# Projections in thirds, one third in each slot of an attention kernel; turned tiles in a bank of their own

## The chip, the cores and the metric

One core of one Trainium2 chip. The metric is the device time of one execution in microseconds (us). Engines are named as in the profile: PE (TensorE), DVE (VectorE), ACT (ScalarE), POOL (GpSimd), SP (SyncE, which here only issues transfers).

## What is computed

A gated cross-attention block and a gated feed-forward block behind it, all in float32. Cut to what matters here:

```
q = concat(ctx, layernorm(x)) @ Wq              # B=8, T=256, 1024 -> 512: 32 heads of 16
k = layernorm(x) @ Wk ; ssm_k = ctx @ Wsk       # 8 key heads, each for G=4 query heads
v = layernorm(x) @ Wv ; ssm_v = ctx @ Wsv
s = q @ [ssm_k, k].T / 4 + alibi, masked to the last 64 positions, of both kinds of keys
x = x + tanh(g_xattn) * (softmax(s) @ [ssm_v, v] @ Wo)
x = x + tanh(g_ffn) * ffn(layernorm(x))         # router, top 4 of 128, 8 blocks of gate/up, shared part
```

## The kernel before

Each float32 operand of a product is split into two parts, `hi` and `lo`, and each product is done in three passes (`PASSES`: hi x hi, lo x hi, hi x lo). ACT makes the high half by a copy, DVE or POOL the low half by a subtraction. So a projection tile is 12 or 24 products on PE.

All engines follow one order written out by hand: a loop over slots, `for n in range(SLOTS)`. A batch has 32 slots (`UNITS`), 4 (`NB`) for each of 8 groups of heads. In slot n PE makes the scores of unit n (`scores`, tile `ps_scores`), and 14 slots later (`LAG`) the same scores turned (`scores_turned`, `ps_scoresT`) for the softmax; DVE takes the row maxima (`maxima`, `neg_max`), which PE turns (`turn_max`) in the third slot after a group's last, which ACT copies (`max_out`, `max_rows`) and sends into the last rows of `q_stack` (`stack_max`). ACT takes the exponentials. The products with the values (`times_v`, tile `ps_o`, 32 small ones) come in every fourth slot. DVE turns their result (`o_turn`, `o_blocks`), POOL divides by the sums.

The work for the next batches hangs on constants that name a slot relative to a batch's first: `PREP` turns rows of ctx and of the normalised x on PE (`prep`, 4 tiles a batch; halves by `prep_high` and `prep_low`, the latter DVE's `actT_lo`), `K_PROJ`, `Q_PROJ` (4 tiles of 24 products), `V_PROJ`, `TURN_V`, `TIMES_WO` (2 tiles of 12 products of 512 columns, one batch later), `TURN_X` (the new x, called x1, turned for the feed-forward part). Each of these jobs takes one of the two banks of `ps_proj` in turn (`take_bank`), and waits until the job two before has been read out (semaphore `pj_done`). `scores(n)` waits for the maxima of slot n - 2 (`max_done`).

Keys and queries then go to where the scores read them: `keep_k` and `keep_q` write them to DRAM (`k_kept`, `q_kept`; each is three transfers, one for each pass), and `stack_k`, `stack_q` read them into `k_stack` and `q_stack` in another layout. Only groups 0 and 1 of batch 0 go directly from `qT` to `q_stack` (`stack_q_first`, `DIRECT = 2`). The other rows of the stacks are written once, by ACT (`key_rows_out`, `query_rows_out`), for groups 3 to 7 in slots 0 to 8 (`FILL_ROWS`). The queries of batch 1 are projected in slots 3, 6, 9 and 12.

The first batches' projections stand ahead of the loop; their weights are split in twelve pieces (`halves`) as they arrive, ten low halves on DVE and two on POOL. From slot `END` = 256 on the feed-forward part follows.

## Time and profile before

| | us |
|---|---|
| median of 3 runs | 975.49 (972.8 to 976.08) |
| profiled execution | 969.84 |
| its span, first to last instruction | 968.0 |
| PE busy | 905.6 (94%) |
| DVE / POOL / ACT busy | 568.6 / 486.6 / 408.3 |
| mean granted clock of PE | 0.991 of full speed |

The profile is of one execution, the runs are timed apart. Busy time of PE counts overlapping matmuls as drawn, so a busy PE isn't one at its peak. A line number is that of the instruction, which can stand in a helper: L1574 is every product of `product`, L1653 the scores, L1672 the turned scores, L1685 the products with the values.

### The profile page before, as it was taken

The page shows a single profiled execution, that of the slowest core. Times are in us where ns is not written, and L with a number is a line of the kernel's source. Part 1 is how long each engine was busy: PE and PEld are TensorE (multiplying, and loading weights), DVE is VectorE, ACT ScalarE, POOL GpSimd, SP SyncE. Part 2 cuts the span into 40 slices and gives each one's busy share as a digit, 9 for nine tenths or more (in the row PEclk, how much of TensorE's full clock was granted, in tenths as well). Part 3 has the DMA queues.
Part 4 walks back from the last instruction along what each step waited for, and adds up shares of the span by engine and source line. Part 5 has one row for each costly group of instructions (what it writes and reads, how often), then busy time and mean ns, then how long its engine had stood idle before and what let it go on. Part 6 is the DMA issues. An engine that isn't in the chain of part 4 may idle for free.

```text
span 968.0 us, 17729 instructions
## 1 busy us (share of the span) xinstructions
PE 905.6 (94%) x6744; PEld 773.7 (80%) x6744; DVE 568.6 (59%) x1117; ACT 408.3 (42%) x858; POOL 486.6 (50%) x531
## 2 busy tenths in 40 slices
PE   6869999999998999989998998899999999999998
PEld 6768978888887989867786786678888888888886
DVE  5357575666667575666122673865655556565657
ACT  4655444353544444454401514334443444444431
POOL 1123061513324151316120999965778888887841
PEclk9899999999999999999999999999999999999999
DMA  6695567473847565499010114450111111202036
GB/s 225 172 188 166 124 163 200 130 202 114 203 125 207 115 171 145 138 254 278 2 44 0 44 44 154 140 183 27 66 66 44 66 54 34 87 22 66 23 98 250
DMA packets 80422, 117.01 MB, mean 121 GB/s; under 512 B 6345, under 2 KB 49098, under 8 KB 79306
## 3 DMA queue, kind: packets, MB, share of 16 engines
q1 hardware_dynamic: 78592, 115.11, 41.9%
q8 instruction: 54, 0.88, 0.4%
q10 hardware_dynamic: 1746, 0.77, 0.4%
q14 instruction: 30, 0.25, 0.1%
HBM read 77.13 MB, written 37.81 MB: 119 GB/s over the span
## 4 chain that ended last, share of the span: by engine, by line
PE 79%; DVE 10%; DMA 3%; issue 3%; ACT 2%; POOL 2%; SPq 1%; ACTq 0%; DVEq 0%; POOLq 0%
PE ps_proj L1574 19%; PE ps_scores L1873 18%; PE ps_scoresT L1873 9%; PE ps_scores L1574 6%; PE ps_o L1685 5%; PE ps_proj L1873 4%; PE ps_scores L1653 4%; PE ps_scoresT L1574 4%; PE ps_scoresT L1672 4%; DMA q_stack<-max_rows 2%; DVE actT_lo L1208 2%; DVE neg_max L1243 2%; DVE o_blocks L1261 1%; DMA q_kept<-qT_hi 1%; PE ps_o L1574 1%
## 5 line engine op out<-in xcount | busy, mean ns | idle before, releaser
L1243 DVE TENSOR_REDUCE neg_max<-ps_scores 128x2 f32<-128x384 f32 (+1 forms) x256 | 128.6, 513 | 136.4 <-PE ps_scores L1653 134.6
L925 ACT ACTIVATE probsT<-ps_scoresT 128x512 f32<-128x512 f32 (+1 forms) x256 | 134.8, 542 | 148.1 <-PE ps_scoresT L1672 144.7
L1653 PE MATMUL ps_scores<-k_stack,q_stack 114*128 114x192 f32 (+1 forms) x512 | 104.8, 289 | 11.5 <-DVE neg_max L1243 7.9
L1134 ACT ACTIVATE part_sums<-ps_scores 128x512 f32<-128x512 f32 x96 | 57.5, 599 | 130.8 <-PE ps_scores L1873 130.8
L1672 PE MATMUL ps_scoresT<-q_stack,k_stack 116*128 116x256 f32 x448 | 103.9, 303 | 9.0 <-DMA q_stack<-max_rows 6.7
L1653 PEld LDWEIGHTS ps_scores<-k_stack,q_stack 114*128 114x128 f32 x512 | 80.4, 193 | 24.9 <-DVE neg_max L1243 15.7
L674 POOL TENSOR_TENSOR o_normal<-o_blocks,inv_sums 128x128 f32<-128x128 f32 x64 | 25.8, 404 | 147.7 <-DVE inv_sums L1263 147.7
L809 POOL TENSOR_TENSOR w_expert_lo<-w_sums,w_expert_hi 128x256 fp32r<-128x256 f32 x64 | 63.8, 1009 | 45.5 <-ACT w_expert_hi L1054 45.5
L821 POOL TENSOR_TENSOR big<-big,basis 128x512 f32<-128x512 f32 x56 | 77.5, 1402 | 14.9 <-DVE basis L1524 14.9
L1672 PEld LDWEIGHTS ps_scoresT<-q_stack,k_stack 116*128 116x128 f32 x448 | 71.5, 194 | 12.3 <-DMA q_stack<-max_rows 7.6
L680 POOL TENSOR_TENSOR oT_lo<-oT_raw,oT_hi 128x256 fp32r<-128x256 f32 x32 | 23.6, 736 | 110.5 <-ACT oT_hi L934 110.5
L1685 PE MATMUL ps_o<-probsT,v_ones 128*32 128x128 f32 (+1 forms) x2048 | 64.2, 267 | 0.5 <-issue 0.5
L1574 PE MATMUL ps_proj<-actT_hi,wq_hi 128*128 128x256 f32 x224 | 64.7, 289 | 0.0
L1574 PE MATMUL ps_proj<-actT_lo,wq_hi 128*128 128x256 f32 x224 | 64.0, 286 | 0.0
L1574 PE MATMUL ps_proj<-actT_hi,wq_lo 128*128 128x256 f32 x224 | 63.9, 285 | 0.0
L1515 DVE TENSOR_TENSOR basis<-part_sums,silu_gate 128x512 f32<-128x512 f32 x32 | 24.2, 756 | 67.2 <-ACT silu_gate L1142 67.2
L1685 PEld LDWEIGHTS ps_o<-probsT,v_ones 128*32 128x32 f32 x2048 | 53.5, 112 | 9.5 <-issue 1.0
L1524 DVE TENSOR_TENSOR basis<-basis,big 128x512 f32<-128x512 f32 x56 | 57.2, 1021 | 1.0
L1494 DVE TENSOR_TENSOR part_sums<-part_sums,ps_scoresT 128x512 f32<-128x512 f32 x32 | 22.0, 688 | 53.6 <-ACT part_sums L1134 53.6
L809 POOL TENSOR_TENSOR w_expert_lo<-w_raw,w_expert_hi 128x256 fp32r<-128x256 f32 x48 | 46.3, 978 | 7.1 <-ACT w_expert_hi L1054 7.1
L1873 PE MATMUL ps_scores<-xnT_hi,w_expert_hi 128*128 128x512 f32 x128 | 49.8, 389 | 0.0
L1873 PE MATMUL ps_scores<-xnT_hi,w_expert_lo 128*128 128x512 f32 x128 | 49.8, 389 | 0.0
(265 smaller groups left out, 2549.7 us busy)
## 6 DMA issues: line engine op xcount, KB each, us to landing
k_stack<-k_kept SPq DMA_DIRECT2D x64, 192.0 KB, 5.2
q_stack<-q_kept SPq DMA_DIRECT2D x31, 384.0 KB, 5.4
q_kept<-qT_hi SPq DMA_DIRECT2D x16, 512.0 KB
big<-coeff_rows SPq DMA_DIRECT2D x8, 1024.0 KB, 4.7
xn_rows<-in_x SPq DMA_DIRECT2D x8, 512.0 KB, 4.2
k_kept<-kT_hi SPq DMA_DIRECT2D x16, 256.0 KB
q_kept<-qT_lo SPq DMA_DIRECT2D x8, 512.0 KB
x_rows<-in_x SPq DMA_DIRECT2D x8, 512.0 KB, 5.3
```

The lines of the kernel that those rows point to most:

```text
L674: pool.tensor_tensor(ON[:, p % 2, :, odd * D:(odd + 1) * D], OB[:, n % 2, :, 0:D], RI[:, n % 2].unsqueeze(2).broadcast_to([P, T // 32, D]) ...
L809: pool.tensor_tensor(WS[n % 2]["lo"][:, w, :], w_source(n, w), WS[n % 2]["hi"][:, w, :].bitcast(F32), ALU.subtract).then_inc(e_lo, 1)
L821: pool.tensor_tensor(dst, dst, BS[:, j, :], ALU.add).then_inc(acc_done, 1)
L925: act.activation(PT[:, g % 2, 2 * j:2 * j + blocks].rearrange("p h f r w -> p (h f r w)"), ST[:, n % 2, 0:blocks].rearrange("p h n -> p (h ...
L1134: act.activation(TP[:, u % 2, j, :], src[:, u % 2, :], ACT.Copy).then_inc(taken, 1)
L1243: dve.tensor_reduce(NM[:, g % 2, 2 * i:2 * i + 2], SA[:, n % 2, :, 0:keys], AX.X, ALU.max, negate=True).then_inc(max_done, 1)
L1524: dve.tensor_tensor(dst, BS[:, j, :], cB[:, k % 2, group_columns(t)], ALU.mult).then_inc(basis_done, 1)
L1574: ins = pe.matmul(out, stat(s, c), mov(m, c), start=c == cs[0] and j == 0, stop=c == cs[-1] and j == PARTS - 1)
L1653: ins = pe.matmul(SA[:, n % 2, f, 0:2 * (near.stop - near.start)], QS[0:TOP, g, i, f].rearrange("p r w -> p (r w)"), keys[:, near, :].rear ...
L1672: ins = pe.matmul(ST[:, n % 2, v, :], KS[0:ROWS, g, j + v, 1 - v].rearrange("p w s -> p (w s)"), QS[0:ROWS, g, j + v].rearrange("p f r w - ...
L1685: ins = pe.matmul(PO[32 * r:32 * r + 2 * D, j * W:j * W + cols_j], VA[:, j, g, :], PT[:, n % 2, 2 * j:2 * j + cols_j // W, :, r, :].rearra ...
L1873: ins = pe.matmul(bank[:, u % 2, :], WS[n % 2][s][:, w, c * P:(c + 1) * P], operand(MEETS[w], m, c, g), start=first and c == 0 and j == 0, ...
```

## The change

K, V, each query tile and each Wo tile are cut into three parts (`third`, `keys_values_third`), and the tables give each part a slot of its own, so that in full batches each of the 24 slots without products with the values has one part. The context is handed over turned (a transposition of the input array on the host), so that ctx needs no `prep`; its halves are made by ACT (`ctx_high`) and POOL (`ctx_low`; DVE for batches 0 and 1). Everything that PE turns (`prep`, `turn_v`, `turn_x`) now uses one bank `PT_`, the former bank of the turned maxima, with a semaphore `turn_done` (batches 0 and 1 use a bank of `ps_proj` beside it); the turned maxima `PM` go into the second half of the bank of `ps_o`, with two new waits. All groups of batch 0 are stacked directly. The rows of the stacks are written by ACT and POOL ahead of the loop. DVE's statistics of x1 come one slot after the residual. The last batch keeps its Wo tiles whole. PE begins with seven products on a tile of ones (`warm`).

```diff
-LOAD_ROWS, STATS = -59, (-46, -45)
-PREP, K_PROJ, Q_PROJ, V_PROJ = (-32, -31, -30, -29), (-27, -26), (-24, -22, -19, -16), (-7, -5)
+LOAD_ROWS, STATS = -64, (-51, -50)
+CTX_HIGH, CTX_LOW = (-44, -43), (-43, -42)
+PREP, K_PROJ, V_PROJ = (-42, -38), (-35, -34, -32), (-15, -14, -12)
+Q_PROJ = ((-31, -30, -28), (-27, -26, -24), (-23, -22, -20), (-19, -18, -16))
+LEAD = (PV - NM_TURN) // NB + 1
-TURN_V, TIMES_WO, TURN_X = 15, (52, 55), (62, 63)
+TURN_V, TIMES_WO, LAST_WO = 16, ((53, 54, 56), (57, 58, 60)), ((52,), (55,))
+def x_turn_slot(b, t):
+    return (69, 72)[t] if b < B - 1 else (62, 64)[t]
...
-    PO, PM = POB[:, 0, :], PNM[0:4 * NB, 1, 0:P]
+    PO, PM = POB[:, 0, :], POB[0:4 * NB, 1, 0:P]
+    PT_ = PNM[:, :, :].rearrange("p h n -> p (h n)")
...
+        def third(out, stat, mov, count, part):
+            steps = [(c, s, m) for c in range(count) for s, m in PASSES]
+            size = len(steps) // 3
+            for i in range(part * size, (part + 1) * size) if part is not None else range(len(steps)):
+                c, s, m = steps[i]
+                ins = pe.matmul(out, stat(s, c), mov(m, c), start=i == 0, stop=i == len(steps) - 1, skip_group_check=True)
+            return ins
...
+        def warm():
+            ones = VA[:, 0].rearrange("p g e -> p (g e)")
+            pe.wait_ge(ones_set, 1)
+            for _ in range(WARM):
+                pe.matmul(PJ[:, 1, 0:T], ones[:, 0:P], ones[:, 0:T], start=True, stop=True)
+
+        def take_turn(*job):
+            kind, b, t = job
+            if kind == "prep" and b < 2 and t == 1:
+                if b == 1:
+                    pe.wait_ge(pj_done, passed("v", 0, 0))
+            elif TURNS[job] >= 1:
+                pe.wait_ge(turn_done, TURNS[job])
+            return turn_place(*job)
...
         def turn_max(n):
             pe.wait_ge(nm_lo, n + 1)
             if n >= 1:
                 pe.wait_ge(nm_out, n)
+            if n > LEAD - 1:
+                pe.wait_ge(o_turned, n - LEAD + 1)
...
         def times_v(n):
-            pe.wait_ge(pj_done, passed("turn_v", b, 0))
+            pe.wait_ge(turn_done, passed("turn_v", b, 0))
             pe.wait_ge(exp_done, NB * (n + 1))
             if n >= 1:
                 pe.wait_ge(o_turned, n)
+            pe.wait_ge(nm_out, min(n + LEAD, GROUPS))
...
+        warm()
         keys_values("k", 0, 0)
-        first_queries(range(HC))
-        prep(0, 2)
-        prep(0, 3)
-        keys_values("k", 0, 1).then_inc(k_mm, 1)
+        first_queries(range(HC - 1))
+        for t in range(TB):
+            prep(0, t)
+        first_queries(range(HC - 1, HC))
+        keys_values("k", 0, 1)
+        for i in range(2):
+            keys_values("v", 0, i)
         first_queries(range(HC, 2 * HC))
...
-        for g in range(DIRECT):
+        for g in range(HK):
             stack_k(0, g)
             stack_q_first(g)
-        keep_q(0)
+            if g == 3:
+                for n in range(FIRST_O, len(halves)):
+                    weight(n)
                 keep_k(1)
...
+    ctx = np.asarray(inputs["ctx_2048"]).transpose(0, 2, 1).reshape(B, HC, P, T)
+    inputs["ctx_2048"] = ctx.transpose(0, 2, 1, 3)
```

How the order moves at three places. First PE, where a batch begins in the slot loop, before: three slots of the four with a `prep` each (`ctx_rows` and `xn_rows` turned into `ps_proj`), no products of a projection between.

```order
L1597 MATMUL ps_proj<-ident,ctx_rows 128x128 [waits ctx_in,pj_done]
L1597 MATMUL ps_proj<-ident,ctx_rows 128x128 x3
L1653 MATMUL ps_scores<-k_stack,q_stack 128x192 [waits max_done]
L1653 MATMUL ps_scores<-k_stack,q_stack 128x192
L1672 MATMUL ps_scoresT<-q_stack,k_stack 128x256 [waits exp_done]
L1597 MATMUL ps_proj<-ident,ctx_rows 128x128 [waits ctx_in,pj_done]
L1597 MATMUL ps_proj<-ident,ctx_rows 128x128 x3
L1653 MATMUL ps_scores<-k_stack,q_stack 128x192 [waits max_done]
L1653 MATMUL ps_scores<-k_stack,q_stack 128x192
L1672 MATMUL ps_scoresT<-q_stack,k_stack 128x256 [waits exp_done,max_in5]
L1672 MATMUL ps_scoresT<-q_stack,k_stack 128x256
L1662 MATMUL ps_o_max<-ident,max_halves 16x128 [waits nm_out,nm_lo]
```

After, one whole slot, 26 of a batch ahead, and the first rows of the next (`wo_hi`, `wo_lo` by `oT_hi`, `oT_lo` are products with Wo, four to a third; `ps_o_max` is now the turned tiles' bank, and the turned maxima go to `ps_o`).

```order
L1781 MATMUL ps_scores<-k_stack,q_stack 128x192 [waits max_done]
L1781 MATMUL ps_scores<-k_stack,q_stack 128x192
L1802 MATMUL ps_scoresT<-q_stack,k_stack 128x256 [waits exp_done,max_in3]
L1802 MATMUL ps_scoresT<-q_stack,k_stack 128x256
L1792 MATMUL ps_o<-ident,max_halves 16x128 [waits o_turned,nm_out,nm_lo]
L1712 MATMUL ps_o_max<-ident,xn_rows 128x128 [waits xn_done,turn_done]
L1712 MATMUL ps_o_max<-ident,xn_rows 128x128 x3
L1676 MATMUL ps_proj<-wo_hi,oT_lo 128x512
L1676 MATMUL ps_proj<-wo_lo,oT_hi 128x512
L1676 MATMUL ps_proj<-wo_hi,oT_hi 128x512
L1676 MATMUL ps_proj<-wo_hi,oT_lo 128x512
L1781 MATMUL ps_scores<-k_stack,q_stack 128x192 [waits max_done]
```

The four turned tiles became two, which stand four slots apart, and a third of a projection now stands behind one of them in the same slot.

Second DVE, at the same place before: its queue has a low half `actT_lo` between the maxima of each of four slots.

```order
L1208 TENSOR_TENSOR actT_lo<-ps_proj,actT_hi 128x4x128 [waits prep_hi]
L1243 TENSOR_REDUCE neg_max<-ps_scores 128x2 [waits s_mm]
L1269 STREAM_TRANSPOSE oT_raw_73<-o_normal 128x256 [waits oT_lo,o_done]
L1208 TENSOR_TENSOR actT_lo<-ps_proj,actT_hi 128x4x128 [waits prep_hi]
L1243 TENSOR_REDUCE neg_max<-ps_scores 128x2 [waits s_mm]
L1208 TENSOR_TENSOR actT_lo<-ps_proj,actT_hi 128x4x128 [waits prep_hi]
L1250 CAST max_halves<-neg_max 128x8 [waits nm_t,max_done]
L1252 TENSOR_TENSOR max_halves<-neg_max,max_halves 128x8 [waits nm_hi]
L1243 TENSOR_REDUCE neg_max<-ps_scores 128x2 [waits nm_lo,s_mm]
L1261 STREAM_TRANSPOSE o_blocks<-ps_o 128x256 [waits o_done,pv_mm]
L1263 RECIPROCAL inv_sums<-o_blocks 128x8 [waits o_turned]
L1208 TENSOR_TENSOR actT_lo<-ps_proj,actT_hi 128x4x128 [waits prep_hi]
```

After, from the slot of the first Wo residual on (`x_rows` is the residual, `x_stats` its statistics).

```order
L1324 TENSOR_REDUCE neg_max<-ps_scores 128x2 [waits s_mm]
L1358 SCALAR_TENSOR_TENSOR x_rows<-ps_proj,tanh_gates,x_rows 128x512 [waits wo_mm,x1_in]
L1324 TENSOR_REDUCE neg_max<-ps_scores 128x2 [waits s_mm]
L1350 STREAM_TRANSPOSE oT_raw_74<-o_normal 128x256 [waits oT_lo,o_done]
L1364 BN_STATS x_stats<-x_rows 128x6 [waits pj_done]
L1366 BN_AGGR x_mean_var<-x_stats 128x2 [waits x1_st]
L1324 TENSOR_REDUCE neg_max<-ps_scores 128x2 [waits s_mm]
L1289 TENSOR_TENSOR actT_lo<-ps_o_max,actT_hi 128x4x128 [waits prep_hi]
L1331 CAST max_halves<-neg_max 128x8 [waits nm_t,max_done]
L1333 TENSOR_TENSOR max_halves<-neg_max,max_halves 128x8 [waits nm_hi]
```

The low halves `actT_lo` moved four slots apart, and the residual's statistics moved behind the maxima of the next slot.

Third SP's queue of transfers ahead of the loop, before: groups 0 and 1 go directly, then all queries are spilled and the others read back.

```order
L476 DMA k_stack<-k_kept 48x4x256 [waits k_rows_set,pad_kept,k_kept]
L483 DMA q_stack<-qT_hi 16x1024 [waits q_rows_set,pj_done]
L483 DMA q_stack<-qT_lo 16x1024
L483 DMA q_stack<-qT_hi 16x1024
L466 DMA q_kept<-qT_hi 8x16x1024 [waits pj_done]
L466 DMA q_kept<-qT_lo 8x16x1024
L466 DMA q_kept<-qT_hi 8x16x1024
L494 DMA q_stack<-q_kept 48x2x1024 [waits q_rows_set,q_kept]
L476 DMA k_stack<-k_kept 48x4x256 [waits k_rows_set,pad_kept,k_kept] x2
L460 DMA k_kept<-kT_hi 8x16x512 [waits pj_done]
L460 DMA k_kept<-kT_hi 8x16x512
```

After, the same place, from group 1 on.

```order
L527 DMA k_stack<-k_kept 48x4x256 [waits rows_pool,pad_kept,k_kept]
L534 DMA q_stack<-qT_hi 16x1024 [waits rows_pool,pj_done]
L534 DMA q_stack<-qT_lo 16x1024
L534 DMA q_stack<-qT_hi 16x1024
L527 DMA k_stack<-k_kept 48x4x256 [waits rows_act,pad_kept,k_kept]
L534 DMA q_stack<-qT_hi 16x1024 [waits rows_act,pj_done]
L534 DMA q_stack<-qT_lo 16x1024
L534 DMA q_stack<-qT_hi 16x1024
```

The spill and the loads back of batch 0 are gone; each group now has one load of keys and three of queries.

## Rows read from the trace of the kernel before

**Rows 1.** The page, part 1: busy time by engine, share of the span, instructions.
```profile
PE 905.6 (94%) x6744; PEld 773.7 (80%) x6744; DVE 568.6 (59%) x1117; ACT 408.3 (42%) x858; POOL 486.6 (50%) x531
```

**Rows 2.** Windows cut at each 32nd slot: stretch, length, busy by engine, clock, DMA.
```profile
core 0: us, PE busy (x) PEld busy (x) DVE busy (x) ACT busy (x) POOL busy (x), PEclk, DMA share, GB/s
0.00:40.70 40.70, 29.86 (x200) 28.12 (x201) 19.41 (x36) 22.40 (x41) 7.88 (x20) 0.96 0.68 203
...
40.70:87.60 46.90, 36.77 (x357) 33.46 (x355) 26.38 (x66) 27.31 (x60) 12.78 (x16) 0.93 0.74 184
...
195.60:249.90 54.30, 51.23 (x583) 46.49 (x582) 35.19 (x91) 24.29 (x55) 17.83 (x28) 1.00 0.61 162
...
412.70:455.90 43.20, 37.03 (x423) 31.15 (x422) 27.17 (x74) 22.18 (x52) 15.55 (x24) 0.92 1.04 271
...
455.90:968.00 512.10, 494.65 (x2292) 402.02 (x2290) 286.88 (x400) 191.08 (x377) 349.31 (x312) 1.00 0.22 73
```

**Rows 3.** Timeline of PE, the scores that open five slots: start us, us, instruction.
```profile
208.47 0.44 PE L1653 MATMUL ps_scores<-k_stack,q_stack 114*128 114x128 f32 x2
...
211.89 0.37 PE L1653 MATMUL ps_scores<-k_stack,q_stack 114*128 114x192 f32 x2
...
212.24 0.36 PE L1653 MATMUL ps_scores<-k_stack,q_stack 114*128 114x192 f32 x2
...
215.68 0.37 PE L1653 MATMUL ps_scores<-k_stack,q_stack 114*128 114x192 f32 x2
...
217.14 0.44 PE L1653 MATMUL ps_scores<-k_stack,q_stack 114*128 114x128 f32 x2
```

**Rows 4.** Chain of waits, three runs of PE in that batch: start us, us, what.
```profile
209.19 2.86 PE ps_proj L1574 x24
...
236.08 2.99 PE ps_proj L1574 x12
...
247.45 0.44 PE ps_proj L1699 x4
```

**Rows 5.** The same chain, the first of four DVE passes on turned tiles.
```profile
252.41 0.52 DVE actT_lo L1208
```

**Rows 6.** DVE by line, 195.6 to 249.9 us: xcount, busy us, mean ns, idle before.
```profile
L1243 DVE TENSOR_REDUCE neg_max<-ps_scores 128x2 f32<-128x384 f32 (+1 forms) x32 | 16.2, 514 | 18.2 <-PE ps_scores L1653 18.1
...
L1208 DVE TENSOR_TENSOR actT_lo<-ps_proj,actT_hi 128x512 fp32r<-128x512 f32 x4 | 2.7, 664 | 0.0
```

**Rows 7.** Timeline of PE: two early products, then the first scores.
```profile
10.32 0.41 PE L1574 MATMUL ps_o<-actT_hi,wkv_lo 128*128 128x256 f32 x1
...
10.53 0.41 PE L1574 MATMUL ps_o<-actT_lo,wkv_hi 128*128 128x256 f32 x1
...
40.74 0.59 PE L1653 MATMUL ps_scores<-k_stack,q_stack 114*128 114x128 f32 x4
```

**Rows 8.** Timeline of SP's queue: direct load; last spill of queries, first load back, twice.
```profile
34.08 0.58 SPq L483 DMA_DIRECT2D q_stack<-qT_hi  x1
...
38.68 2.66 SPq L466 DMA_DIRECT2D q_kept<-qT_hi  x1
...
49.54 0.34 SPq L494 DMA_DIRECT2D q_stack<-q_kept  x1
...
228.11 0.61 SPq L466 DMA_DIRECT2D q_kept<-qT_hi  x1
...
241.12 0.33 SPq L494 DMA_DIRECT2D q_stack<-q_kept  x1
```

**Rows 9.** Chain of waits in batch 0, on the turned maxima's transfer.
```profile
60.51 10.16 DMA q_stack<-max_rows
```

**Rows 10.** The page, part 6: transfers, xcount, KB each, us to landing.
```profile
q_stack<-q_kept SPq DMA_DIRECT2D x31, 384.0 KB, 5.4
...
q_stack<-qT_hi SPq DMA_DIRECT2D x4, 64.0 KB, 3.3
```

**Rows 11.** Timeline of ACT, the copy of the turned maxima in the slot from 212.24.
```profile
213.40 0.25 ACT L910 ACTIVATE max_rows<-ps_o_max 16x128 fp32r<-16x128 f32 x1
```

More of the change, by code:

```diff
@@ L567, in _ @@
             if s == 1:
[L568 removed]
+                sp.wait_ge(q_kept, 16 * PARTS * (B - 1))
                 router = cols(a["L0_ffn_w_router"], 0)
@@ new lines, in keys_values_third, with queries @@
+        def keys_values_third(job, b, part):
+            size = 2 * HC * PARTS // 3
+            for src in range(2):
+                steps = range(max(part * size - src * HC * PARTS, 0), min((part + 1) * size - src * HC * PARTS, HC * PARTS))
+                if len(steps):
+                    keys_values(job, b, src, steps)
+        def queries(b, r, part):
+            dst = take_bank("q", b, r) if part == 0 else place("q", b, r)
+            ins = third(dst[:, 0:T], lambda h, c: WQ[h][:, c, r * P:(r + 1) * P], lambda h, c: AT[h][:, c, :], 2 * HC, part)
+            if part == 2:
+                ins.then_inc(q_mm, 1)
@@ L1688, in times_v, with times_wo @@
             ins.then_inc(pv_mm, 1)
-        def times_wo(b, t):
-            dst = take_bank("wo", b, t)
-            pe.wait_ge(oT_lo, HC * (b + 1))
-            product(dst, lambda h, c: OT[h][:, t, c, :], lambda h, c: WO[h][:, c, :], range(HC)).then_inc(wo_mm, 1)
+        def times_wo(b, t, part):
+            first = part in (0, None)
+            dst = take_bank("wo", b, t) if first else place("wo", b, t)
+            if first:
+                pe.wait_ge(oT_lo, HC * (b + 1))
+            ins = third(dst, lambda h, c: OT[h][:, t, c, :], lambda h, c: WO[h][:, c, :], HC, part)
+            if part in (2, None):
+                ins.then_inc(wo_mm, 1)
         def turn_x(b, t):
-            dst = take_bank("x", b, t)
+            dst = take_turn("x", b, t)
             pe.wait_ge(x1_n, TB * b + t + 1)
```

465 lines of the change are left out of this document (252 added, 213 removed).

## Prediction

> **What bounds the kernel now.** I read the page's busy times first. PE is busy for 94% of the span, every other engine for 59% or less [rows 1], so time can only come from PE: from work taken off it, from its gaps, or from its slow clock. The windows then say where the gaps are [rows 2]. I cut them at every 32nd slot, since a batch has 32 slots. From 455.9 us on (512.1 us, PE 97% busy) the diff moves almost nothing, and no gain is to be had. The head, 0 to 40.7 us, has PE busy for 29.86. Batch 0's slots, 40.7 to 87.6, have 36.77 of 46.90. From 87.6 to 412.7 the batches are alike: 54.3 us, PE 51.23 (one stands in the rows, six there are, 325.1 us together). Batch 7's slots take 43.2 with 37.03 busy, at a clock of 0.92.
>
> A busy PE in such a row isn't PE at its peak, because a matmul that waits in the pipe is drawn longer. So I price a slot from the starts of its first scores [rows 3]. Where products stand between (208.47 to 211.89) the slot takes 3.42 us, of which the 24 products are 2.86 [rows 4]: 0.56 is left. The next slot has no product, 0.35. The next, with 24 products and the turned maxima, is 3.44, so 0.58 without them. The fourth, with the products with the values (PV below), is 1.46. That is 2.95 for a group of four slots, 23.6 for a batch. Here PE was never held up. A batch has 24 products for the keys, 24 for the values, 96 for the queries: 144 at 2.86/24 = 0.119 us are 17.2. The 24 with Wo, twice 2.99 in the chain [rows 4], are 6.0. Turned tiles cost 0.44 each [rows 4]; there are seven (four `prep`, the values, two of x1), 3.1. Sum 49.9. Against 54.3, 4.4 us of each batch is waiting. The chain shows for what: four low halves `actT_lo` in a row on DVE [rows 5], each 664 ns beside 514 ns for a slot's `neg_max` [rows 6]. Slots without products are too short for DVE, which then stands idle for 18.2 us of the batch in the long ones [rows 6]. Work is badly spread, it isn't too much.
>
> **The change part by part.**
> *Thirds.* A group has three slots without PV, a batch 24; and K, V, four queries and two Wo tiles in thirds are 24 pieces, one for each. A third of 8 products is 0.95 us, one of Wo's about 1.0. So slots become 1.3 to 1.55 us, and PV's stays at 1.46. DVE has 35.2 us in a batch [rows 2], 1.10 a slot. Its worst new slot (13: maxima, a query's low half, one tile's row statistics) I put at 1.8, the 0.51 and two passes like the 0.66 [rows 6], the next at 1.4; PE asks for the maxima of two slots back, so 0.3 over is hidden. If that cover were gone, each such slot would cost its 0.3, some 1 us a batch.
> *Context turned ahead.* Two `prep` a batch go, 2 x 0.44 = 0.9 us of PE, with ACT's and DVE's two passes from PSUM. In their place ACT reads SBUF, and POOL makes the low half (it has 17.8 of 54.3 us busy; hidden).
> So a batch needs 49.9 - 0.9 = 49.0. I take 49.5 for slots that still meet a wait now and then: 4.8 us off each of five batches, 4.2 off batch 1 (53.7 now, no x1 to turn): **28**. Bounds: 49.0 for all (31), or half of the waits kept, 51.5 (17).
> *Turned tiles in a bank of their own.* Spaced by three slots or more (5, 8, 16, 22, 26), each is emptied by DVE in 0.66 us [rows 6] and by ACT in about as much, long before the next, 4 us later; nothing.
> *Maxima turned into the bank of PV.* `turn_max` now waits for the DVE transpose two slots earlier, and PV for ACT's copy of the maxima turned in the slot before. That copy ended at 213.65 [rows 11], 1.41 us after its slot began at 212.24. In the new order PV stands at 1.53 + 0.46 = 1.99. So 0.6 is left: nothing. If ACT came late, all of PE's queue would stand behind PV, in each of 64 groups.
> Here a rule speaks against the change. The Trainium skill, "PSUM — Partial Sum Buffer", section "PSUM bank collisions raise a hardware error", says that two engines must never be in one bank and quadrant at once and that the hardware doesn't make them take turns, so whoever shares a bank between two uses has to pay in waits on semaphores. The trace of before has each use in its own bank and can't show that price; by the rows it is 0 and the sum stays, by the rule it can be anything that ACT's lateness makes it, which is rival 5.
> *Spill.* From the first spill of the queries to the first load back 13.0 us pass in a batch (228.11 to 241.12), with SP standing in between [rows 8]; the load lands 5.4 later [rows 10]. The spill starts in slot 18 as before. 13.0 + 5.4 = 18.4 us, and slot 32, which needs the load, comes 14 x 1.5 = 21 us after slot 18. It fits by 2 to 3 us, and SP's other work is queued behind.
>
> *Head.* Two of the first products start 0.21 us apart [rows 7], against 0.119 later: the slow level, 1.2 GHz, after PE's waiting. Seven products on ones run before, while nothing else could. 23 products at 0.094 less are 2.2 us. Until the first scores PE now has 168 products, 20.0, and four turned tiles, 1.8, from about 7.2 us: 29.0 if nothing held it. The splits of twelve weight pieces on ACT and then DVE, and x's statistics and normalisation through POOL, do hold it; I add 4.5, between nothing and the 9 that now lie in 0 to 40.7 (PE idle for 10.8 of it [rows 2]), so 33.5 against 40.74 [rows 7]: **7**. Bounds 30 and 38.
> *Batch 0.* The queries no longer go by DRAM: before, 10.9 us lie between last spill and load [rows 8]; a direct load lands in 3.3 [rows 10]. But there are 24 of them and 8 of the keys, at 0.58 us of SP each [rows 8]: 2.4 a group of four slots, faster than the slots need. The four Wo loads and the spill of batch 1's keys come after group 3, some 5 us, and group 4 just makes its slot. ACT's five sets of rows leave these slots. The transfer of the maxima that took 10.16 [rows 9] no longer competes with a spill. PE's own work: slots 0 to 13, ten thirds 9.5 and scores 3.9; slots 14 to 31, 4.5 groups 13.2, seven thirds 6.7, three turned tiles 1.3, and 0.9 for eight slots without a piece, where DVE sets the pace (27.17/32 = 0.85 a slot [rows 2]). 35.5, and 2.5 for transfers: 38 against 46.9: **9**. Bounds 36 and 44.
> *Batch 7.* Wo of batch 6 was 6.0 in two blocks; in slots with DVE as pace its six pieces hide 1.7 behind it. The x1 tiles of batch 6 move behind slot 256, 0.9 here and there: **2**. With DMA at 1.04 of its engines' time [rows 2] another stall may take it.
>
> Sum 28 + 7 + 9 + 2 = **46 us**. The profiled execution is 968.0 + 1.84 = 969.84, the median of the runs 975.49; its lowest is 972.8. I expect 924 for a profile and 975.5 - 46 = 929.5 for the median.
>
> **The rivals.**
> 1. *Forecast*: PE becomes the pace of each slot, 929.5, with 919 to 942 as its range. Chance 0.70.
> 2. *The slots stay paced by hand-offs*: equal slots leave each engine the right mean, but scores wait for maxima in most groups. For: DVE and PE hand over twice a slot. Against: 1.10 of 1.5 us. They give back a third of what is there, 52.5 us a batch: 10 instead of 28 off, 947.5. Chance 0.14.
> 3. *The spilled queries come late*: DMA's share was 0.61 and must rise to 0.67. If spill and load stretch by a third (6 us) against 2 spare, that is 4 a batch for six batches, 24 of the 46 lost: 953.5. Against: the lag grows only if DMA is near its limit, and 0.67 isn't. Chance 0.06.
> 4. *The head is bound by transfers*, weights and stacks, and gives nothing: 16 less, 945. For: share 0.68 and 0.74. Against: 10.9 us of spill go. Chance 0.06.
> 5. *Slower*: PV waits for the copy of the maxima in each of 64 groups. ACT has one queue with exponentials and high halves ahead. It decides from 46/64 = 0.7 us a group, so the copy must come 1.3 us later than 1.41; at 1 us it is 994. Against: ACT is busy 24.3 of 54.3. Chance 0.04.
>
> **How the numbers follow.** This kernel's measurement tells about 0.3%, 3 us, from no change. All but rival 5 are faster beyond it: 0.95; within it 0.02, for a mixture near its threshold; slower 0.03. The likeliest gives 929.5. Its own range is 919 (31 + 11 + 11 + 3 = 56 off) to 942 (22 + 4 + 6 + 1 = 33 off: all four terms near their low bounds). To hold 8 in 10 I go from 918 up to 949, into rivals 2 and 4; above stay rivals 3 and 5, and half of 2.
>
> **What would show it.** Right: windows of 32 slots at 49 to 50 us; four neighbouring slots between 1.3 and 1.6; first scores near 33.5; slot 32 near 71; `actT_lo` no longer in the chain between slots; early products 0.119 apart. Wrong: `max_rows` or `o_blocks` as what PE waits for before PV or turned maxima; `q_stack<-q_kept` before scores; a clock below 1.00 in the batches; 455.9 to the end longer than 513.

## The result and the profile after

| | before | changed |
|---|---|---|
| median of the runs | 974.14 us (972.66 to 976.08) | 937.94 us (937.33 to 941.46) |
| profiled execution, its span | 969.84, 968.0 | 937.33, 935.5 |
| mean granted clock in it | 0.991 | 0.984 |

The ratio of the medians is 0.9635, with a 95% interval from 0.9603 to 0.9667. That is 36.2 us faster. The forecast was 46 us less, 929.5 us; 937.94 lies in the range given, 8.4 us above the forecast.

Of the changed kernel, first the page's busy times, which answer to [rows 1], then the windows that answer to [rows 2]. They are cut at the first scores, at slot 32, at slot 16 of one of the like batches and the same place of the next, at slot 224, and at the first router product (456.23 us before, 417.88 now).

```profile
PE 888.0 (95%) x6694; PEld 767.0 (82%) x6694; DVE 571.5 (61%) x1107; ACT 401.2 (43%) x838; POOL 519.2 (55%) x562
```

```profile
core 0: us, PE busy (x) PEld busy (x) DVE busy (x) ACT busy (x) POOL busy (x), PEclk, DMA share, GB/s
0.00:36.08 36.08, 29.39 (x199) 27.29 (x200) 22.93 (x38) 22.28 (x41) 22.29 (x35) 0.95 0.64 193
36.08:88.37 52.29, 36.65 (x381) 34.66 (x380) 27.04 (x68) 20.32 (x45) 19.13 (x23) 0.87 0.62 155
184.30:232.71 48.41, 48.41 (x578) 45.43 (x573) 35.03 (x89) 24.58 (x55) 20.35 (x30) 1.00 0.69 182
376.44:417.88 41.44, 36.10 (x429) 30.93 (x423) 29.89 (x79) 22.55 (x52) 16.13 (x25) 0.92 1.04 281
417.88:935.50 517.62, 498.78 (x2297) 405.02 (x2295) 285.66 (x398) 191.28 (x377) 353.20 (x318) 0.99 0.22 74
```

Put beside [rows 2] and the first scores of [rows 7], the 32.5 us that the span lost fall out like this:

| stretch | before | changed | gain | forecast |
|---|---|---|---|---|
| head, to the first scores | 40.74 | 36.08 | 4.7 | 7 |
| slots 0 to 31 | 46.9 | 52.3 | -5.4 | 9 |
| slots 32 to 223 | 325.1 | 288.1 | 37.0 | 28 |
| slot 224 to the first router product | 43.5 | 41.4 | 2.1 | 2 (with its 0.9 behind slot 256) |
| from there to the end | 511.8 | 517.6 | -5.8 | 0 |

A like batch now takes 48.41 us and PE is busy for all of it, where [rows 2] has 51.23 of 54.30. The timeline of PE shows the scores that open the slots of one such group, to be read as [rows 3] was (start us, us, instruction):

```profile
184.30 0.44 PE L1781 MATMUL ps_scores<-k_stack,q_stack 114*128 114x128 f32 x2
185.81 0.36 PE L1781 MATMUL ps_scores<-k_stack,q_stack 114*128 114x192 f32 x2
187.11 0.37 PE L1781 MATMUL ps_scores<-k_stack,q_stack 114*128 114x192 f32 x2
188.63 0.37 PE L1781 MATMUL ps_scores<-k_stack,q_stack 114*128 114x192 f32 x2
190.09 0.44 PE L1781 MATMUL ps_scores<-k_stack,q_stack 114*128 114x128 f32 x2
```

The slots are 1.51, 1.30, 1.52 and 1.46 us long, where one was 3.4 and its neighbour 0.35. In the whole chain of waits from 184 to 233 us PE is the only engine.

What PE waited for in the changed kernel, over the whole span, longest sums first (engine, tile, line, releaser: us in total, times, longest):

```profile
PE ps_scores L1781 <- DVE neg_max L1324: 16.7, 5, 13.2
PE ps_proj L1665 <- DVE down_lo L1515: 6.4, 4, 3.3
PE ps_scoresT L1802 <- ACT probsT L999: 3.1, 6, 1.0
PE ps_scores L1757 <- DVE wq_lo L1279: 2.3, 1, 2.3
PE ps_o L1816 <- ACT max_rows L984: 2.1, 6, 0.7
```

One wait of 13.2 us stands out, in batch 0. Three timelines, PE, DVE and SP's queue, show it from its end to its cause (in brackets the idle time before, and its releaser):

```profile
51.59 0.37 PE L1781 MATMUL ps_scores<-k_stack,q_stack 114*128 114x192 f32 x2
65.39 0.66 PE L1781 MATMUL ps_scores<-k_stack,q_stack 114*128 114x128 f32 x2 [13.18 <-DVE neg_max L1324]
```

```profile
50.29 0.41 DVE L1301 TENSOR_TENSOR second_qT_lo<-ps_proj,second_qT_hi 128x256 fp32r<-128x256 f32 x1
63.89 0.69 DVE L1267 BATCH_NORM_STATS2 stats<-xn_rows 128x6 f32<-128x512 f32 x1 [13.19 <-DMA xn_rows<-in_x]
```

```profile
40.56 3.00 SPq L500 DMA_DIRECT2D w_stage<-in_L_xattn_Wo  x4
43.61 1.32 SPq L511 DMA_DIRECT2D k_kept<-kT_hi  x2
...
59.09 0.59 SPq L534 DMA_DIRECT2D q_stack<-qT_hi  x1
59.72 0.58 SPq L504 DMA_DIRECT2D xn_rows<-in_x  x1
```

PE stands ahead of slot 16 (the scores with 128 columns open a group) for DVE's maxima. DVE stands ahead of its statistics of batch 2, which the change moved from slot 18 to slot 13 of this batch. And the rows that they read are asked for only at 59.72, because the load stands last in SP's queue, behind all 32 stack transfers, the four of Wo and the three that keep the keys of batch 1. SP itself is never idle for long here: it needs 0.62 us from one stack transfer to the next where nothing holds it. The sixteen issues from 45.7 us on took 0.87 us each on average, the longest 2.27.

### The profile page after: what moved, and what is told of

The parts are those of the page before. It is cut to its first block, busy times and chain, and to the rows that moved or that the text cites. A ratio compares the mean times of both kernels' runs of the same rounds, so it can differ in the third digit from the quotient of the medians.

```text
span 935.5 us, 17701 instructions
## 1 busy us (share of the span) xinstructions
PE 888.0 (95%) x6694; PEld 767.0 (82%) x6694; DVE 571.5 (61%) x1107; ACT 401.2 (43%) x838; POOL 519.2 (55%) x562
## 4 chain that ended last, share of the span: by engine, by line
PE 84%; DMA 4%; DVE 3%; POOL 3%; SPq 2%; issue 2%; ACT 1%; POOLq 0%; DVEq 0%; ACTq 0%
PE ps_scores L2004 19%; PE ps_proj L1676 12%; PE ps_scoresT L2004 9%; PE ps_scores L1781 6%; PE ps_scoresT L1802 6%; PE ps_scores L1665 5%; PE ps_o L1816 5%; PE ps_proj L2004 5%; PE ps_proj L1665 5%; PE ps_scoresT L1665 4%; PE ps_proj L1730 4%; SPq L534 1%; DMA q_kept<-second_qT_hi 1%; DMA xn_rows<-in_x 1%; POOL x_normal L757 1%
## 5 line engine op out<-in xcount | busy, mean ns | idle before, releaser
L999 ACT ACTIVATE probsT<-ps_scoresT 128x512 f32<-128x512 f32 (+1 forms) x256 | 137.2, 542 | 149.8 <-PE ps_scoresT L1802 149.4
L1324 DVE TENSOR_REDUCE neg_max<-ps_scores 128x2 f32<-128x384 f32 (+1 forms) x256 | 131.5, 516 | 75.5 <-PE ps_scores L1781 71.2
L1781 PE MATMUL ps_scores<-k_stack,q_stack 114*128 114x192 f32 (+1 forms) x512 | 100.5, 280 | 17.5 <-DVE neg_max L1324 16.7
L1781 PEld LDWEIGHTS ps_scores<-k_stack,q_stack 114*128 114x128 f32 x512 | 82.3, 192 | 28.5 <-issue 14.5
L875 POOL TENSOR_TENSOR w_expert_lo<-w_sums,w_expert_hi 128x256 fp32r<-128x256 f32 x64 | 64.3, 1014 | 45.6 <-ACT w_expert_hi L1130 45.6
L1585 DVE TENSOR_TENSOR part_sums<-part_sums,ps_scoresT 128x512 f32<-128x512 f32 x32 | 22.0, 688 | 52.4 <-ACT part_sums L1210 52.4
```

The lines of the kernel that those rows point to most:

```text
L875: pool.tensor_tensor(WS[n % 2]["lo"][:, w, :], w_source(n, w), WS[n % 2]["hi"][:, w, :].bitcast(F32), ALU.subtract).then_inc(e_lo, 1)
L999: act.activation(PT[:, g % 2, 2 * j:2 * j + blocks].rearrange("p h f r w -> p (h f r w)"), ST[:, n % 2, 0:blocks].rearrange("p h n -> p (h ...
L1324: dve.tensor_reduce(NM[:, g % 2, 2 * i:2 * i + 2], SA[:, n % 2, :, 0:keys], AX.X, ALU.max, negate=True).then_inc(max_done, 1)
L1781: ins = pe.matmul(SA[:, n % 2, f, 0:2 * (near.stop - near.start)], QS[0:TOP, g, i, f].rearrange("p r w -> p (r w)"), keys[:, near, :].rear ...
```

## The experiments

Each is the changed kernel with an edit, timed beside the kernel before. "Slot 16 of a batch" is read from PE's turn of the values, which stands there; in the changed kernel that is at 66.4 us for batch 0 and 112.1 for batch 1.

**e1, the rows of batch 2 asked for earlier.**

```diff
             if g == 3:
+                load_rows(2)
                 for n in range(FIRST_O, len(halves)):
...
-            b = due(n, LOAD_ROWS, 2)
+            b = due(n, LOAD_ROWS, 3)
```

> The changed kernel with one edit: the load of the rows and of ctx of batch 2 is issued on SP behind the fourth group's stack transfers, ahead of the four loads of Wo, and no longer behind all 32 stack transfers. Theory A (batch 0 lost its gain to one stall: DVE stands 13.2 us in the statistics of batch 2, in slot 13, for rows whose load SP's queue issues only at 59.7 us): the load is issued near 41 and has landed by 46, before DVE comes to it at 50.7; the 13.8 us row at slot 12/13 goes, slot 32 starts near 75 in place of 88.4, and the time is 925 us (923 to 928). Theory B (what is behind the stall is late anyway: the last stack transfers, now 1.2 us later, and the spilled queries of batch 1, which stand in the chain at 71.7): part of the wait comes back before slot 32, slot 32 starts at 80 or later, and the time is 930 to 936. Theory C (the place of the load makes nothing, DVE is held by something else): 938.

Measured: 932.53 us (928.24 to 934.24), ratio 0.9578 (0.9546 to 0.9611). The profiled execution was its fastest, with a span of 926.4. The 13.2 us wait is gone, and slot 16 of batch 0 comes at 57.3 in place of 66.4, 9.0 earlier. Theory A has the cause, but not the whole price: another wait came up behind it, as B said. The timeline of PE at the same place:

```profile
51.59 0.42 PE L1803 MATMUL ps_scoresT<-q_stack,k_stack 116*128 116x256 f32 x2
56.32 0.69 PE L1782 MATMUL ps_scores<-k_stack,q_stack 114*128 114x128 f32 x2 [4.31 <-DMA q_stack<-qT_hi]
```

Now group 4's queries themselves are late. The windows of this kernel show the 16 DMA engines with little or nothing free meanwhile:

```profile
40.00:46.00 6.00, 6.00 (x54) 6.00 (x53) 3.99 (x10) 0.77 (x3) 0.00 (x0) 1.00 0.85 257
46.00:52.00 6.00, 4.65 (x39) 4.28 (x37) 2.46 (x7) 3.66 (x8) 4.66 (x4) 1.00 0.95 269
52.00:58.00 6.00, 1.69 (x9) 1.68 (x9) 2.97 (x9) 1.02 (x2) 3.89 (x8) 0.69 0.98 161
```

**e2, the statistics back where they were.** The edit is `STATS = (-46, -45)` in place of `(-51, -50)`.

> The changed kernel with the statistics of batches 2 to 7 five slots later on DVE, where the kernel before has them (offsets -46 and -45), and the load left where it is in SP's queue. Theory A (DVE is only too early for the load): slot 18 comes at 36.1 + 18 x 1.46 = 62.4 us, the rows land at 63.9, so 1.5 us of the 13.2 is left; 926.5 us (925 to 930). Theory B (what is behind the rows, the normalisation and the turned tile in slot 22, is then late instead): the stall moves to PE's wait for xn_rows or for turned tiles in slots 22 to 30 and the time is 931 to 937. If the steady batches need the earlier statistics as well, slots 32 to 223 cost more than 288 us.

Measured: 950.15 us (945.52 to 951.8), ratio 0.9758 (0.9722 to 0.9794): 12 us slower than the changed kernel. In batch 0 it did what A said: DVE waits 2.4 us for the rows in place of 13.2, and slot 16 comes at 55.1. But the like batches take 50.80 us each, two of them 52.4, and over the whole span PE waits six times for the normalised rows, 14.0 us together. The timeline of PE shows the place, the turned tile of slot 22:

```profile
117.11 1.09 PE L1712 MATMUL ps_o_max<-ident,xn_rows 128*128 128x128 f32 x4 [2.19 <-POOL xn_rows L746]
117.85 0.78 PE L1676 MATMUL ps_proj<-wo_hi,oT_lo 128*128 128x512 f32 x1
118.42 0.63 PE L1676 MATMUL ps_proj<-wo_lo,oT_hi 128*128 128x512 f32 x1
```

Since the change turns the tile in slot 22, the statistics must stand as early as they do, or GpSimd's normalisation is late. After the 2.19 us of waiting here PE also runs at its slow level: from 117.1 to 120.6 the granted clock is 0.52. So the early statistics are not a slip: only their load was forgotten.

**e3, the thirds undone.** All three thirds in the slot that holds the last, so K at -32, the queries at -28, -24, -20, -16, V at -12, Wo at 56 and 60.

> The changed kernel with each projection whole again: all three thirds in the slot that now holds the last of them (K at -32, the queries at -28, -24, -20, -16, V at -12, Wo at 56 and 60); DVE's placing, the bank for turned tiles and the loads stay. Theory A (the thirds are what makes the steady batches fast: a whole projection costs PE 2.5 us in one slot while DVE's 1.3 us of maxima a slot can't be caught up in the slots without): six batches take near 325 us as before in place of 288, time 965 to 980. Theory B (the dealing of DVE's work and the bank of its own give it, the thirds little): below 945. Between (each gives a part): 945 to 965; the sum of slots 32 to 223 tells the share.

Measured: 966.57 us (965.78 to 966.66), ratio 0.9933 (0.991 to 0.9956). A like batch takes 52.07 us, of which PE is busy for 50.05. Theory A holds by the time, though slots 32 to 223 take 313 us and not near 325. Without the thirds 3.66 of the 5.86 us that the change takes off each batch (54.27 to 48.41) are gone. The other 2.2 stay, and come from what e3 leaves in: the context that needs no turning, DVE's placing, the bank for turned tiles. No run takes these apart. PE also waits for ACT's copy of the maxima ahead of the products with the values 35 times in e3, 7.8 us together, where the changed kernel has 2.1, so it is beside the thirds that this shared bank is cheap.

**e4, no warm-up.** `WARM = 0` in place of 7.

> The changed kernel with no warm-up products. My prediction's term was 2.2 us saved by them. Theory A (they save nearly that): 940 us, first scores at 38.3. Theory B (PE waits 2.3 us for wq_lo behind the keys' products, the granted clock falls again there and 16 products at 0.21 us follow in either case, so they only save the half speed of the first 12 products, 12 x 0.09 = 1.1 us, which the wait for wq_lo then swallows): 938 us within 0.5, first scores at 36.1 to 36.6.

Measured: 939.69 us (937.62 to 940.1), ratio 0.9652 (0.9623 to 0.9681), not to be told from the changed kernel. The time alone is nearer to A's, but the first scores start at 35.9 us in place of 36.1, so theory B holds for the head, and slot 16 of batch 7 still starts 0.35 us earlier than in the changed kernel. The two profiled executions are 2.5 us apart; all of it comes later, 1.5 between slot 16 of batch 7 and the first router product (21.2 us, 19.7 in the changed kernel) and 1.3 from the shared down projection on, which the edit doesn't touch. In the changed kernel the first twelve products come 0.12 us apart, then PE waits 2.32 us for `wq_lo`, and the products behind it are 0.21 apart again until 14.4:

```profile
7.03 0.36 PE L1730 MATMUL ps_o<-actT_hi,wkv_hi 128*128 128x256 f32 x1 [1.12 <-DVE actT_lo L1284]
11.02 0.58 PE L1757 MATMUL ps_scores<-actT_hi,wq_hi 128*128 128x256 f32 x1 [2.32 <-DVE wq_lo L1279]
```

Without the warm-up the twelve stand 0.21 apart, from 7.14 to 9.62, and the queries' products follow at 9.84 without that wait. Neither order brings the first scores forward.

**e5, the turned tiles close together.** Offsets -39, -38 in place of -42, -38, and 71, 72 in place of 69, 72; the statistics of x1 in the slot of the residual.

> The changed kernel with its thirds, but DVE's work no longer spread: the two turned tiles of a batch stand in neighbouring slots again (offsets -39, -38 and 71, 72 in place of -42, -38 and 69, 72), and the statistics of x1 stand in the slot of the residual. Whole projections gave 52.07 us per batch (before 54.27, changed 48.41), so 2.2 us of the 5.9 gained per batch is not the thirds'. Theory A (it is the spreading of DVE's work): two or three slots of each batch become 0.6 to 1.5 us longer, steady batches at 49.5 to 51, time 946 to 955. Theory B (it is the bank of its own for what is turned and the earlier statistics, and DVE has room in every slot beside thirds): 48.4 to 48.7 per batch, time 937 to 940. Two turned tiles in neighbouring slots share the one bank, so the second one can also wait for DVE's low part of the first: up to 1.4 us a pair, as the pair behind slot 256 shows.

Measured: 959.37 us (958.57 to 960.56), ratio 0.9852 (0.9832 to 0.9873). 51.76 us a batch, 3.35 more and over what A allowed. The waits of PE from 115 to 330 us, some four batches, are these two, and nothing else:

```profile
PE ps_o_max L1708 <- DVE actT_lo L1289: 6.2, 4, 1.5
PE ps_o_max L1830 <- DVE xs_lo L1370: 5.6, 4, 1.4
```

11.8 us in four batches are 2.95 each, nearly the whole loss. The second of two tiles stands behind the first because both use the one bank, and it stands until ACT and then DVE have emptied it. How long that is depends on what DVE has ahead. Here the first tile was turned at 176.89 and ACT had its half at 178.13, but DVE made the low half only behind the residual, its statistics, maxima and a transposition:

```profile
177.42 0.74 DVE L1358 SCALAR_TENSOR_TENSOR x_rows<-ps_proj,tanh_gates,x_rows 128x512 f32<-128x512 f32 x1
179.82 0.65 DVE L1289 TENSOR_TENSOR actT_lo<-ps_o_max,actT_hi 128x512 fp32r<-128x512 f32 x1
```

PE came to the second tile near 179.0 and waited 1.54 us. Had DVE begun at 178.13, the bank would have been free near 178.8, by my estimate, before PE came. In the other pair (the tiles of x1, at 149.0) DVE began 0.5 us behind ACT, and 0.9 of its 1.4 us would be left. So the edit shows the one bank and DVE's lumps together. What either costs alone it doesn't tell.

**e6, the last tile in another bank.**

```diff
+        if job == ("x", B - 1, 1):
+            return PJ[:, JOBS["wo", B - 1, 0] % 2, :]
```

> The changed kernel, with the very last turned tile (x1 of batch 7, second tile) in a free projection bank and not in the one bank for turned tiles. Theory A (of the 6.4 us that the part behind slot 256 costs more than before, 1.4 is PE's wait for the low part of the first tile, because both use one bank): that wait goes, the last router products start 1.4 us earlier, 936.5 us, a difference near what can be measured; the trace shows it as 42.9 to 43.2 us from the first shared product to the last router product in place of 44.5. Theory B (the tiles come no earlier, PE waits for the normalised rows then): 44.5 stays.

Measured: 935.50 us (932.54 to 938.51), ratio 0.9606 (0.9577 to 0.9636). From the first shared product to the last router product 43.4 us pass; the same reading of the changed kernel is 44.9 (that of the expectation ends one product group earlier). By the trace theory A holds; by the times alone this kernel can't be told from the changed one. In the changed kernel each of two steps has its wait, first for the bank, then for the tile:

```profile
475.80 0.60 PE L1834 MATMUL ps_o_max<-ident,x_normal 128*128 128x128 f32 x4
477.81 0.66 PE L1834 MATMUL ps_o_max<-ident,x_normal 128*128 128x128 f32 x4 [1.41 <-DVE xnT_lo L1370]
479.88 0.50 PE L1665 MATMUL ps_scores<-xnT_hi,w_router_hi 128*128 128x512 f32 x1 [1.41 <-DVE xnT_lo L1370]
```

DVE and ACT had nothing else to do here, so 2.0 us from tile to tile, 1.4 of them waiting, is what the one bank costs by itself. In e6 the second tile follows at once:

```profile
475.21 0.60 PE L1838 MATMUL ps_o_max<-ident,x_normal 128*128 128x128 f32 x4
475.65 0.60 PE L1838 MATMUL ps_proj<-ident,x_normal 128*128 128x128 f32 x4
```

**e7, the head reordered.** The load of batch 0's rows behind the first two halves of Wq, and DVE's `weights_low(1)` and `(2)` ahead of its first statistics.

> The changed kernel with the head reordered: the load of batch 0's rows stands behind the first two halves of Wq on SP, and DVE makes the low parts of these two before the statistics of the rows. In the changed kernel PE waits 2.32 us at 8.7 for wq_lo, and its clock falls. Theory A (this wait and the fallen clock are the 2.6 us by which the first scores at 36.1 miss my 33.5): query products start near 9 at 0.12 us apart, first scores at 33.8 to 34.8, time 936. Theory B (the rows, their normalisation and the turned tiles set the head, as the 1.93 us wait for xn_rows at 29.9 and the wait behind the first three query chunks say): the gain is waited away before the turned tile of batch 0 near 17, first scores at 36 or later, time 938 to 939.

Measured: 938.50 us (936.05 to 940.72), ratio 0.963 (0.9599 to 0.9662): no difference. The wait for `wq_lo` is gone and the 36 early query products end at 13.0, but then PE waits for the rows:

```profile
15.28 0.63 PE L1715 MATMUL ps_o_max<-ident,xn_rows 128*128 128x128 f32 x4 [1.95 <-DVE xn_rows L1275]
```

The first scores come at 36.55. Theory B holds: the head goes by the rows' way through statistics, roots, normalisation and splits.

**e8, the queries of batch 0 through DRAM as before** (groups 2 to 7).

> The changed kernel with the queries of batch 0 for groups 2 to 7 taken through DRAM, as the kernel before does, and not straight from SBUF: 18 transfers of 64 KB go, 3 of 512 KB to DRAM and 6 of 128 KB back come. Theory A (what the load of batch 2's rows waits for in SP's queue is the number of issues at about 0.62 us): 18 less, 9 more, so the load is issued 5.6 us earlier and the stall of DVE is 7.5 us in place of 13.2, provided the queries are back in time; slot 16 of batch 0 near 61, time 932 to 934. Theory B (the way through DRAM costs what the kernel before showed, some 10 us until the first queries are back, and SP stands in that wait with everything behind it): PE stands before slot 8 for a query stack, and the stall of DVE is as long as before, time 938 to 944.

Measured: 946.57 us (944.57 to 950.92), ratio 0.9735 (0.9702 to 0.9767), 8.6 us slower than the changed kernel. Theory B has the place, PE's stand for a query stack, but DVE's stall is 9.8 us, between the 7.5 of A and the 13.2 of B, and the time lies 2.6 us above B's range. PE's waits from 36 to 110 us:

```profile
PE ps_scores L1790 <- DVE neg_max L1333: 10.5, 3, 9.8
PE ps_scores L1790 <- DMA q_stack<-q_kept: 6.3, 1, 6.3
```

So the direct transfers are a gain in spite of the stall behind them.

**e9, SP's order by need.** Stacks 0 to 3, Wo, the rows of batch 2, stacks 4 and 5, its context, stacks 6 and 7, and `keep_k(1)` last.

> The first experiment took the stall of DVE away (13.8 us) and brought 9.0 us by slot 16: a 4.3 us wait for the query stack of group 4 came up behind it, with the 16 DMA engines busy 85 to 98 per cent from 40 to 58 us. Here the order on SP is: stacks of groups 0 to 3, Wo, rows of batch 2, stacks of groups 4 and 5, ctx of batch 2, stacks of groups 6 and 7, and only then the keys of batch 1 to DRAM. So 1.25 MB (ctx and the kept keys) no longer stand ahead of group 4. Theory A (what counts is only the bytes and issues ahead of each group's stack): 1.25 MB at the 250 GB/s of that stretch is 5 us, group 4 lands before its slot, slot 16 of batch 0 starts 12 to 13 us earlier than in the changed kernel (53.5 to 54.5), time 924 to 928. Theory B (the DMA engines are full either way, the wait moves to group 5 or 6 or to the kept keys and queries of batch 1): slot 16 of batch 1 stays near 103.5 as in the first experiment, time 930 to 933.

Measured: 934.12 us (933.2 to 934.66), ratio 0.9591 (0.9572 to 0.9611). Slot 16 of batch 0 comes at 54.6, 11.8 us earlier and next to what A expected. But slot 16 of batch 1 comes at 104.2, where e1 had 103.5: B holds, with a time 1.1 us above its range. PE stands 4.0 us shortly ahead of slot 32 for ACT's `probsT`, because ACT stands 5.3 us ahead of the first rounded half of oT, for the second queries to be in DRAM (they lie where oT is written). The chain of waits (start us, us, what):

```profile
63.47 11.63 DMA q_kept<-second_qT_hi
...
75.18 0.10 ACT oT_hi L1015
...
75.50 0.59 ACT probsT L1004
...
76.23 0.77 PE ps_scoresT L1807 x2
```

**e10, that first half six slots later.** `o_high(0)` and `o_low(0)` in slot 33, with e9's order.

> The order on SP of the last experiment (e9), and the first step of batch 0's turned outputs (the rounded half of oT, ACT and GpSimd) six slots later, in slot 33. In e9 ACT stood 5.3 us there, until 75.1, for the second queries to be in DRAM, because they lie where oT is written, and PE stood 4.0 us for probsT behind it. Theory A (that wait is what gave back the gain): no wait for probsT, 46.1 us or less from slot 16 to slot 48 in place of 49.6, time 928 to 931, near 928.5. Theory B (the transfers of this stretch are late altogether, the keys of batch 1 too): another wait in its place, 49 us stay, time 933 to 935.

Measured: 932.85 us (931.06 to 935.97), ratio 0.9594 (0.9571 to 0.9617). Theory B, by the trace: the wait for `probsT` is gone and another is in its place, ahead of slot 32, the first of batch 1, and from slot 16 to slot 48 it takes 51.5 us, more than the 49.6 of e9. SP's queue and PE's timeline:

```profile
60.09 0.61 SPq L519 DMA_DIRECT2D q_kept<-second_qT_hi  x1
...
73.28 0.34 SPq L544 DMA_DIRECT2D q_stack<-q_kept  x1
```

```profile
71.97 0.37 PE L1790 MATMUL ps_scores<-k_stack,q_stack 114*128 114x192 f32 x2
78.16 0.66 PE L1790 MATMUL ps_scores<-k_stack,q_stack 114*128 114x128 f32 x2 [4.67 <-issue]
```

**e11, e10 and e6 together.**

> e10 with the last turned tile in a free projection bank, which took 1.5 us of PE's waits by itself. Expected is e10 less 1.5 us: 926 to 929.5. Rival: the terms don't add, within 0.5 us of e10.

Measured: 930.28 us (926.75 to 932.07), ratio 0.956 (0.9538 to 0.9583). By the medians it is the fastest version, 7.7 us under the changed kernel, and 2.6 under e10, 0.8 above the range expected; e1 (0.9546 to 0.9611) can't be told from it.

**e12, the four small loads behind the queries of batch 1.** `TANH - 20` in place of `TANH - 24`, with e11.

> e11 with the four small loads (gates, amplitudes, scale) issued on SP behind the queries of batch 1 and no longer ahead of them; they take SP's queue 3.9 us, from 57.2 to 61.1. In the four kernels without the first stall (e1, e9, e10, e11) slot 48 starts at 103.5 to 104.7, whatever stands ahead; in e10 and e11 PE stands 4.7 and 6.2 us ahead of slot 32, whose queries went to DRAM at 60 to 65 us, were there at 73.5, and came back near 78. Theory A (the way of the queries of batch 1 through DRAM sets slot 32): they are issued 3.5 us earlier, slot 32 starts 2.5 to 3.5 us earlier (75 to 76 in place of 78.5), slot 48 at 101 to 102, time 927 to 928. Theory B (the stacked keys of batch 1, issued at 65.1 and landed near 74.8, and the full DMA engines set it too): less than 1 us is gained, 929.5 to 930.5.

Measured: 930.43 us (929.05 to 935.56), ratio 0.9571 (0.9544 to 0.9597). The queries are issued 3.9 us earlier, at 57.2, but are back for loading only at 72.4 in place of 73.8; slot 32 starts at 77.3 in place of 78.5. Nearer to B: the way through DRAM has only stretched. It isn't full transfer engines that stretch it: from 58 to 76 us their busy share is 0.61 here, 0.55 in e11 and 0.63 in e10. What holds it is open.

The start of slot 32 of all five without the first stall, from PE's timeline: e1 79.8, e9 80.5, e10 78.2, e11 78.5, e12 77.3, against 88.4 in the changed kernel. Between 8 and 11 us came out of the 13.2, and the medians show only 3.8 to 5.4 of it (e1, e9, e10). In some traces part of the rest is lost in the stretch from slot 16 of batch 6 to the first router product, which all these kernels have alike and where the transfer engines are busy for 0.85 to 0.88. It takes 63.7 us in the changed kernel's trace, 62.6 in e1's, 65.8 in e9's, 64.3 in e10's, and 67.9 in e11's and e12's. The windows of e1 and e12, and PE's longest wait in e12's:

```profile
345.70:408.30 62.60, 56.17 (x672) 48.99 (x671) 46.22 (x121) 32.70 (x75) 19.67 (x32) 0.97 0.88 236
```

```profile
PE ps_scoresT L1815 <- DMA q_stack<-max_rows: 3.2, 1, 3.2
```

```profile
345.10:413.00 67.90, 58.91 (x673) 51.33 (x672) 46.25 (x121) 32.73 (x75) 19.74 (x32) 0.92 0.85 219
```

PE waits up to 3.2 us for the 8 KB of turned maxima in e12's trace and 0.4 in e1's, and the granted clock is 0.92 against 0.97. Executions of one kernel differ by 1.5 us (e9) to 6.5 us (e12), and the differences between the medians of e1, e9, e10 and e12 stay inside that. That this late transfer is what makes them differ is not shown, since each kernel has one trace.

## Why the prediction was right, and where it was not

The main mechanism, thirds that make PE the pace of each slot, is right. That the total lies in the range is in part luck: 9 us too little for the thirds stand against 14.4 too much for batch 0, 2.3 for the head and 5.7 for batch 7 and what follows.

**Thirds, 28: right, and too small; 37.0 measured.** That PE is now the pace is shown by PE busy for 48.41 of 48.41 us, and that the thirds bring most of it by e3 (3.66 of 5.86 us a batch; the rest is not taken apart). The sum of 49.0 was 0.6 too high: a third of Wo took 0.92 to 0.94 and not 1.0, which is 0.4 of it. The 0.5 that I added for slots that still meet a wait wasn't needed. That is 1.1 us in each of the batches from 64 on. Slots 32 to 63 gained 6.2 (53.7 to 47.5) where I took 4.2, and slots 192 to 223 take only 46.90: the tiles and the first two thirds of the keys, which the change moves ahead into the batch before, have no next batch there, 1.5 more. 5.4 + 2.0 + 1.5 is nearly the 9 that the term was short. Rival 2, pace by hand-offs, is out by the same rows. So is rival 3: in the like batches PE waits for no spilled query, with the transfer engines busy for 0.69.

**"Turned tiles in a bank of their own ... nothing": right, on the condition that was named.** Spaced by three slots or more the bank is free in time; in neighbouring slots, with DVE's work in lumps as well, it costs 3.35 us a batch (e5). At the end of the last batch, where I didn't look, nothing spaces them: that is the 1.5 us of e6.

**Rival 5, PV behind the copy of the maxima: 2.1 us.** It is in the list of waits, six times, 0.7 at most, where 0.7 in each of 64 groups would have been needed to lose. The Trainium skill, "PSUM — Partial Sum Buffer", section "PSUM bank collisions raise a hardware error", leaves the keeping apart to the program, so each shared bank is paid for in semaphore waits; the trace agrees, with 2.1 us for PV's bank, and 2.95 us a batch in e5 for the one of the turned tiles. The prediction says that the trace of before can't show such a price, and that is wrong: its jobs share the two banks of `ps_proj`, and PE waited five times, 3.0 us together, for DVE's `xs_lo` to give one back.

**Batch 0, 9: wrong by 14.4 us; it lost 5.4.** The step that failed is "2.4 a group of four slots, faster than the slots need ... and group 4 just makes its slot". I priced SP's queue against the stacks alone, and at 2.4 us a group where the last four groups took 3.5. It is in order, and at its end stood the rows of batch 2, which DVE now wanted in slot 13 and not 18. Take the wait of 13.2 off and 39.1 is left, near my 38. But e1 and e9 to e12 show that it isn't to be had so: behind the first wait there is a second, group 4's stack or the queries of batch 1, and 42 to 45 us pass until slot 32. Over PE's own 35.5, my "2.5 for transfers" was 6.5 to 9.5. The rival "transfers" (number 4) put this into the head and the stacks together; it came true for batch 0, and its price of 16 us was about what head and batch 0 together fell short of theirs (16 forecast, -0.7 measured).

**Head, 7: 4.7 measured.** Two parts of the step were wrong. The warm-up, put at 2.2 us, is worth 0 here (e4). And the 4.5 us for what holds PE were 7.1, of which 16 products at 0.21 us behind the wait for `wq_lo` are 1.5. But e7 takes that wait out, and the first scores don't come earlier: the gain is waited away for the rows. So of the 2.6 us between 33.5 and 36.1 the step that failed is the estimate of what holds PE, and the rows' way is what holds it.

**Batch 7 and behind, 2: -3.7 measured.** The text had "455.9 to end longer than 513" as a sign against it, and from the first router product on it is 5.8 us longer. 2.05 of it lie ahead of the first shared product (the two x1 tiles of batch 6, 0.9, and waits of PE that they and `probsT` bring), 1.5 in front of the last router tile, of which e6 takes 1.5 back. The other 2.25 are in the stage of the shared down projection, which the change doesn't touch. There both kernels have the same waits for `down_lo` (7.1 and 6.4 us). The windows, first of the kernel before, then of the changed one:

```profile
577.00:637.10 60.10, 52.87 (x220) 37.91 (x220) 40.89 (x41) 19.87 (x38) 56.17 (x45) 1.00 0.42 137
```

```profile
542.30:604.60 62.30, 55.75 (x220) 40.28 (x219) 40.65 (x41) 20.28 (x39) 56.33 (x45) 0.95 0.39 129
```

The granted clock is 1.00 in one and 0.95 in the other. Behind the 3.3 us wait PE fell to the slow level in the changed kernel (0.72 in the six us from 560.3) and not in the one before. From the start of this stage to the end, 390.0 us before and 392.3 changed, the experiments gave between 391.1 and 394.4. Whether it is chance or the change stays open: of the kernel before there is one trace, and all thirteen of the others lie above it.

## What to carry to other kernels

When a table of slots moves a step on one engine, move its load too, and count the whole of the issuing queue ahead of it, not only the transfers of the same kind. A long wait hides the next one: before a stall's length is entered as the gain of its cure, ask what would be late a few microseconds on (13.2 us here were worth about 5). And work cut into equal pieces pays when two engines hand over each slot, as long as pieces that share one bank stay some slots apart.
